# Windowed attention inside a vision tower: softmax sums and turned scores share a PSUM bank, row maxima one slot earlier, no hardware loop

## Time and profile before

| | |
|---|---|
| device time, 3 runs | 1922.61, 1926.5 (median), 1938.78 us |
| profiled execution, its span | 1920.1 us |
| busy: PE, DVE, POOL, ACT | 73%, 70%, 63%, 57% |
| granted TensorE clock, mean | 0.806 of full |

### The profile page before, as it was taken

One profiled execution on the slowest core, in us unless ns is written; L12 is line 12 of the kernel. 1 busy time (PEld: TensorE's weight loads), 2 busy tenths in 40 slices (PEclk: granted clock), 3 DMA queues, 4 the chain that ended last, 5 costly groups with the idle time before them and its releaser, 6 DMA issues. The chain is left out here.

```text
span 1920.1 us, 31423 instructions
## 1 busy us (share of the span) xinstructions
PE 1396.5 (73%) x8148; PEld 648.9 (34%) x8148; DVE 1341.6 (70%) x1835; ACT 1086.1 (57%) x2020; POOL 1209.0 (63%) x1665
## 2 busy tenths in 40 slices
PE   3765768787969697786869687686868687666565
PEld 1443434343425243243424333242424333121111
DVE  1111688888786857878686867879686877878941
ACT  1234657675565747575475756566575857564432
POOL 2014486867685856767585765768586776967651
PEclk9877979796878878797788878796987978676755
DMA  2001686666565655666465665566566666777820
GB/s 63 1 14 57 162 226 192 195 187 173 159 200 156 182 167 157 189 186 173 138 185 174 165 190 162 174 169 193 150 170 184 172 198 175 213 192 204 222 70 6
DMA packets 214770, 304.52 MB, mean 159 GB/s; under 512 B 78924, under 2 KB 79128, under 8 KB 214424
## 3 DMA queue, kind: packets, MB, share of 16 engines
q1 hardware_dynamic: 214552, 302.09, 55.8%
HBM read 274.75 MB, written 20.97 MB: 154 GB/s over the span
## 5 line engine op out<-in xcount | busy, mean ns | idle before, releaser
L1262 POOL TENSOR_TENSOR hc<-hs,c_rep 128x512 f32<-128x512 f32 x512 | 652.2, 1274 | 461.0 <-DVE hs L1014 458.6
L1014 DVE TENSOR_TENSOR_SCAN hs<-bank,state,xd 128x512 f32<-128x512 f32 x512 | 650.8, 1273 | 83.2 <-issue 57.8
L767 ACT ACTIVATE bank<-dl,a_neg 128x512 f32<-128x512 f32 x512 | 350.3, 687 | 209.7 <-DVE hs L1014 186.7
L1005 DVE TENSOR_TENSOR xd<-xd,bank 128x512 f32<-128x512 f32 x512 | 337.1, 663 | 57.1 <-PE bank L439 53.3
L1032 DVE TENSOR_REDUCE neg_max<-bank 128x8 f32<-128x512 f32 x128 | 88.1, 688 | 281.1 <-PE bank L528 272.6
L538 PE MATMUL bank<-q_diag,k_heads 128*128 128x128 f32 x1024 | 226.4, 348 | 6.0 <-ACT shift L760 4.5
L538 PEld LDWEIGHTS bank<-q_diag,k_heads 128*128 128x128 f32 x1024 | 193.8, 229 | 82.8 <-issue 65.5
L775 ACT ACTIVATE probsT<-bank 128x512 f32<-128x512 f32 x128 | 76.4, 597 | 256.1 <-PE bank L539 255.6
L528 PE MATMUL bank<-k_heads,q_diag 128*128 128x512 f32 x256 | 175.1, 772 | 56.3 <-DMA q_diag<-rot 25.5
L449 PE MATMUL bank<-hc,wts 128*32 128x512 f32 x1024 | 182.8, 777 | 4.0 <-POOL hc L1262 2.6
L1334 POOL TENSOR_TENSOR ew<-ew,e 128x512 f32<-128x512 f32 x96 | 121.4, 1264 | 64.9 <-ACT e L760 64.8
(11 more groups left out here) (176 smaller groups left out, 2493.3 us busy)
## 6 DMA issues: line engine op xcount, KB each, us to landing
xd<-xdel_rows SPq DMA_DIRECT2D x512, 256.0 KB, 4.1
dl<-delta_rows SPq DMA_DIRECT2D x512, 256.0 KB, 3.8
delta_rows<-delta SPq DMA_DIRECT2D x16, 512.0 KB, 6.3
xdel_rows<-xdel SPq DMA_DIRECT2D x16, 512.0 KB, 3.1
xin<-in_x_dram SPq DMA_DIRECT2D x32, 128.0 KB, 2.4
q_diag<-rot SPq DMA_DIRECT2D x32, 128.0 KB
out_dram<-res SPq DMA_DIRECT2D x256, 16.0 KB
k_heads<-rot SPq DMA_DIRECT2D x128, 16.0 KB
```

The costliest lines, as they stand in the source:

```text
L767: act.activation(decay_ps[n % 2][:, :], dl[:, n % 4, :], ACT.Exp, scale=a_neg[:, g:g + 1])\
L1005: dve.tensor_tensor(xd[:, n % 8, :], xd[:, n % 8, :], b_ps[:, :], ALU.mult).then_inc(injected.sem, 1)
L1014: dve.tensor_tensor_scan(hs[:, n % 4, :], decay_ps[n % 2][:, :], xd[:, n % 8, :], state[:, g:g + 1], ALU.mult, ALU.add).then_inc(scanned.s ...
L1262: pool.tensor_tensor(hc[:, n % 8, :], hs[:, n % 4, :], c_rep[:, BAND * h:BAND * h + BAND], ALU.mult)\
```

## The change

In A_USES bank 4 now holds only the scores S0 to S7 (besides the uses before and after the windows), and bank 5 holds T0 P0 T1 P1 ... The table AT moves max to slot 10 + 2w and has an entry of its own for shift, which stays at 11 + 2w. DVE gets a wait before max: neg_max has two buffers, so max(w) waits for shift(w-2). The loop is gone: all 21 rounds are written out. With it go the product in place of a transpose (turn) and the two small extra products (L466, L694).

```diff
-A_USES = [("xT", 0), ("k", 1), ("q", 0), ("k2", 1), ("q2", 0), ("v0", 0), ("v1", 1), ("S0", 0), ("S1", 0)]
+A_USES = [("xT", 0), ("k", 1), ("q", 0), ("k2", 1), ("q2", 0), ("v0", 0), ("v1", 1)]
+A_USES += [(f"S{_w}", 0) for _w in range(NW)]
 for _w in range(NW):
-    A_USES += [(f"P{_w}", 0)] + ([(f"S{_w + 2}", 0)] if _w + 2 < NW else [])
-A_USES += [(f"T{_w}", 1) for _w in range(NW)] + [("oT", 0), ("proj", 1)]
+    A_USES += [(f"T{_w}", 1), (f"P{_w}", 1)]
+A_USES += [("oT", 0), ("proj", 1)]
...
-AT = {"S": [9 + 2 * _w for _w in range(NW)], "max": [11 + 2 * _w for _w in range(NW)],
+AT = {"S": [9 + 2 * _w for _w in range(NW)], "max": [10 + 2 * _w for _w in range(NW)],
+      "shift": [11 + 2 * _w for _w in range(NW)],
...
-        def run(eng, body):
-            for c in range(-3, 3):
-                body(c, c % 2)
-            with eng.Fori(3, NCH - 4, 2) as c:
-                body(c, 1)
-                body(c + 1, 0)
-            for c in range(NCH - 3, NCH + 2):
+        def rounds(body):
+            for c in range(-3, NCH + 2):
                 body(c, c % 2)
...
-                pe.matmul(uses[0].bank[0:32, 0:8], col("y_sel", 0, 32), xT[:, 0:8], start=True, stop=True)
...
-                        last = turn(use.bank[:, 128 * i:128 * i + 128], xin[:, 2 * i:2 * i + 2, :], ident, i == 0)
+                        last = pe.transpose(use.bank[:, 128 * i:128 * i + 128], xin[:, 2 * i:2 * i + 2, :], ident)
...
-                pe.matmul(uses[0].bank[0:32, 0:8], col("y_sel", 0, 32), e1[:, 0, 0:8], start=True, stop=True)
...
-                if s in AT["max"]:
-                    w = AT["max"].index(s)
+                if s in AT["shift"]:
+                    w = AT["shift"].index(s)
                     act.wait_ge(A[f"S{w}"].drained, A[f"S{w}"].empty(k))
...
                     use = A[f"S{w}"]
                     dve.wait_ge(use.filled, use.full(k))
+                    if w > 1 or past(k - 1):
+                        dve.wait_ge(shift_ready.sem, shift_ready.at(k, w - 1))
                     dve.tensor_reduce(neg_max[:, w % 2, :], use.bank[:, :].rearrange("p (h j) -> p h j", h=HEADS),
```

More of the change, by code:

```diff
@@ L93, in at @@
     def at(self, chunk, k):
-        value = chunk * self.per + k
-        return max(value, 0) if isinstance(value, int) else value
+        return max(chunk * self.per + k, 0)
 class Use:
@@ L267, in past @@
         def past(k):
-            return not isinstance(k, int) or k >= 0
+            return k >= 0
         def group(n):
@@ L275, in has @@
         def has(k):
-            return not isinstance(k, int) or 0 <= k < NCH
+            return 0 <= k < NCH
         def ahead(c, n, k):
@@ L420, in _ @@
                 lo, hi = COL["rw2"]
-            run(sp, body)
+            rounds(body)
             sp.wait_ge(stored.sem, stored.at(NCH - 1, 256))
@@ L426, in _ @@
             ident = col("ident")
[L428 to L431, removed]
             def spread_b(k, q, h):
@@ L563, in prepare @@
                         for i in range(4):
-                            last = turn(use.bank[0:64, 128 * i:128 * i + 128], xn[:, 4 * i2 + i, :], ident, i == 0)
+                            last = pe.transpose(use.bank[0:64, 128 * i:128 * i + 128], xn[:, 4 * i2 + i, :], ident)
                         last.then_inc(use.filled, 1)
@@ L751, in _ @@
             pe.wait_ge(setup_act, 2)
-            run(pe, body)
+            rounds(body)
         @block.scalar
@@ L995, in _ @@
             act.wait_ge(setup_dve, 11)
-            run(act, body)
+            rounds(body)
         @block.vector
@@ L1226, in _ @@
             dve.wait_ge(setup_pool, 13)
-            run(dve, body)
+            rounds(body)
         @block.gpsimd
@@ L1363, in _ @@
             pool.wait_ge(setup_dve, 11)
-            run(pool, body)
+            rounds(body)
 def pack(v):
```

## The result

| | before | after |
|---|---|---|
| device time, median of 4 runs | 1924.55 us (1908.23 to 1938.78) | 2015.24 us (2014.98 to 2017.49) |
| ratio, 95% interval | | 1.052 [1.048, 1.057] |
| span and mean granted clock of the profiled execution | 1920.1 us, 0.806 | 2012.4 us, 0.766 |

The changed kernel is 5.2% slower. The forecast was 1938.5 us with a range up to 1966; the time lies 49 us above that range. Some executions of a kernel run longer than the rest at a lower clock; a ratio compares only executions without that, a median takes in all.

What follows compares the result with a forecast made beforehand. PE bounds the attention stretch, DVE slots 14 to 20. Loop -24, early windows -6, steady chunks +46, chunk 3 +5, small products -7, gaps before S -2: +12 us, so 1938.5 us, range 1884 to 1966.

Steps and rivals of the forecast that it cites:

- The maxima: Attention windows: maxima ahead of the odd slot's scan delay decay, exp and P; +4.1 us per steady chunk.
- the +46 of the sum: Twelve steady chunks (4 to 15) at 4.1 us of new waiting less 0.3 for half-clock windows.
- Rival 3: PE's clock pattern shifts: four more chunks at the low level +23 us, six fewer -35; chance 0.10, half each.
- The loop: Slots 30 to 0: PE's branch back and the gap after it go, -24 us (14 to 30).
- the small products: L466, L694 and the product in place of a transpose go: -5 us in steady rounds, -2 in the others.
- P's bank: S(w+2) no longer waits 0.33 us for pv(w): -6 us early, about 12 x 0.7 more if the new wait is covered.
- rival 1: Attention stretch: the new wait on DVE's scan is covered, so the kernel gets faster, 1881 us; chance 0.22.
- The early rounds: Rounds -3 to -1: six windows of three chunks gain 0.33 us each from P's own bank, -6 us.
- Rival 2: DVE's chain paces every attention window, L664 and L707 also late, loop gives only 14: 1957 to 1977 us; chance 0.22.

Runs made afterwards that it cites:

- 1872 us version: The kernel before with all rounds written out, small extra products gone and P in T's bank, maxima still in slot 11 + 2w: 1872.09 us, ratio 0.980.
- the old banks: Two runs with banks as before, all rounds written out: maxima in their old slot 1926.13 us, maxima one slot sooner 2015.51 us.
- the fillers: The changed kernel with unread PE products ahead of P1, P5 and P6: 1901.68 us, ratio 0.993; with those ahead of P1 alone 1912.48 us.
- the filler ahead of P6: An unread 128x384 PE product ahead of P6, added to the changed kernel together with those ahead of P1 and P5: 1901.68 us.
- The long hold: The 1872 us version with two added ACT copies (128x960, 128x512) ahead of exp of window 1: 1967.84 us, ratio 1.026.
- the three pairs: Loop against written-out rounds, in us: old banks and maxima 1924 and 1926; P's bank alone 1875.55 and 1872.09; both moves 2034.97 and 2015.
- The holds: The 1872 us version with added ACT copies ahead of exp of window 1: one copy 1865.87 us, two copies 1967.84 us.
- the filler in the second layers: The kernel with maxima behind the scan of slot 10 + 2w (1845 us), plus an unread 128x512 product ahead of each experts' second layer: 1879.81 us.

## Why the prediction was wrong

**The maxima.** The mechanism was right in each part: the order on DVE, the decay behind the scan, exp behind the decay, P1, P5, P6 and T7 late, P2 to P4 covered. The term failed by its size. "Per steady chunk: 1.6 - 0.1 - 0.33 + 1.1 + 1.8 = +4.1 us" was idle time of PE priced as if the work around it kept its speed. From the 1872 us version to the changed kernel a round grew by 11.2 us (116.0 - 104.8): 2.3 us are idle time (25.9 - 23.6), less than forecast, and 9.0 are PE's busy time (90.2 - 81.2) for the same instructions, which ran at half speed for longer. With the old banks the split is 4.2 idle and 3.5 slower.

The lateness itself seems priced about right. With the fillers in, the late chain and the filler ahead of P6 cost 58 us together, 16 from S2 to S3 and 42 from S6 on, against the +46 of the sum. What went with the fillers is 82 us from S3 to S6 (325.9 - 244.0), more than the 54 that the move had brought there (325.9 - 272.0), and 29 us from S6 on (701.0 - 671.7). The long hold makes the same kind of loss from S3 to S6 by the gap at P1 alone, 96 us in all (1968 - 1872). For the stretch from S6 on no run has the gaps without the move, so there the share of the clock rests on the fillers alone. Rounds 0 and 1 (S7 to S7) lost 8 and 11 us against the 1872 us version, where 5 and 4 were forecast.

**The clock.** Rival 3 had the right mechanism with too small a price and chance: four chunks more at the low level, +23 us, chance 0.05 for that sign. It took 24.7 us as the low case of S3 to S6; seven of the twelve steady chunks now take 29.1 to 29.6. Over the eight rounds PEclk fell from 0.84 to 0.77. I had kept both signs because the earlier trace rows show a dense stretch that falls without a gap. The Trainium skill (TensorE: Matmul & The Clock Gate, HAM oscillation) says that idle gaps bring the clock down. The holds and the fillers agree with it for the gap at P1: 1.66 us, low in all twelve chunks; 1.90, in eleven; 0.18, in none. They also show that it isn't the whole story: 1.24 us were harmless in sum, and the filler in the second layers made the kernel slower.

**The loop.** Forecast -24, and -7 for the small products; measured -3.5, +2 and -20 us in the three pairs. No run separates the loop from these products. Where the loop is, from S2 of chunk 5 to S2 of chunk 15, the written-out traces are shorter by 21 us (1068.0 for 1089.0), 14 and 31 (1158.1 for 1188.8), so the term fits there. In the first two pairs it is lost again outside, at a lower clock in the second, and between one execution and the next. One reading of the prediction was off: the best spacing of S7 in that trace is 104.3 us (829.16 - 724.87), and both spacings of 105.9 are of looped rounds without a branch back, not of straight-line code.

**P's bank.** Forecast -14 in rival 1; measured -49 with the loop, -54 without it, -77 with the maxima behind the scan, 0 with early maxima. The early rounds gave 8 to 10 us and not 6: the first scan starts at 198.4 us, not 207.9, with the loop, and at 197.9, not 205.7, without. Loop, small products and P's bank together were forecast at -45 (the 1881 us of rival 1) and measured at -52, by two errors that cancel; that is luck.

**Rival 2** (L664 and L707 late in w3 and w4 too) came nearest in time, 1957 to 1977, 38 us short and by the wrong mechanism: from S3 to S6 PE has no idle time at all in one of the two windows after and 0.6 us in the other.

**What stays open.** Why a gap of 1.24 us lowers the clock in some rounds and one of 1.9 us in nearly all, and how far it depends on what stands before it, isn't settled; no run here varies the work ahead of a fixed gap. A gap of 1.90 us left the full clock in chunk 4, and one of 1.03 us was followed by either level in one and the same trace. Nor is it shown why P's bank acts so strongly on the clock, since its waits are only 0.33 us each.

## What to carry over

Where PE is nearly always busy, a few us of waiting per round can cost far more than they last (here a round with 2.3 us more idle time grew by 11.2), because the work behind the wait slows down: compare PE's busy time for equal instruction counts and the granted clock before trusting a sum of waits. A test is cheap: put useless products into the new gap, and if the time falls, it was not the wait alone that cost. If it rises, as in the second layers here, nothing is shown about the gap. And here the maxima, which wait for PE, belonged behind DVE's ready scan and not ahead of it: one swapped pair was worth 170 us.

## What the hardware showed

- Filler products whose result nobody reads made the changed kernel 103 us faster (2015.24 to 1912.48).
- 0.66 us more of one wait per round made a kernel 102 us slower (1865.87 to 1967.84); 0.89 us more before that (0.35 to 1.24) had cost nothing.
- A pause of 5.3 us in a window left its length unchanged (23.1 against 22.9 us), since the clock was 0.95 and not 0.70.
- The same gap of 1.03 us before P1 was followed by a clock of 0.57 to 0.59 in three chunks and of 1.00 in nine.
